# Attention outputs reach the output projection's layout through DRAM, with one inverse denominator row per head spread to 16 rows

## The chip, the cores and the metric

The kernel is one program on one core of a Trainium2 chip. Its time is the device time of one execution in microseconds (us). Before the change three runs gave 2191.11, 2204.84 and 2227.48 us; the median is 2204.84 us. The core has five engines that run their own instruction streams in order: TensorE (PE; its weight loads are shown apart as PEld), VectorE (DVE), ScalarE (ACT), GpSimd (POOL) and SyncE (SP, which here only issues transfers). They meet through semaphores.

## The reference, cut to what matters

The input is x of 4 batches, 1024 rows and 512 columns, all in float32. The block is a causal attention and then a mixture of experts, each between layer norms:

```python
# attention: 32 query heads of 16 columns, 8 key/value heads (each serves 4 query heads)
q, k = rope(x @ Wq), rope(x @ Wk);  v = x @ Wv
probs = softmax(causal(q @ k.T / sqrt(16)))
out = (probs @ v).transpose(0, 2, 1, 3).reshape(B, S, 512)    # head h is columns 16h .. 16h+15
attn = out @ Wo
x = x + layernorm(attn(layernorm(x)))
x = x + layernorm(moe(layernorm(x)))     # 64 experts, top 6, and a shared expert
```

The change concerns the two lines in the middle: the division of probs @ v by the sum of the exponentials, and the layout in which its result meets Wo.

## The kernel before, in words

The program has three phases: attention with everything that hangs on one row tile (out projection, layer norms, router, shared expert, dispatch of rows to experts), then 64 experts, then a final sum and layer norm. Only the first is touched. It ends about 1705 us into the execution.

Its attention works on 64 **items**: one batch, one half of its 512 query rows each, one key/value head with its four query heads. Per item, in order: SP loads the group's rotated rows (`load_group`, L613); ACT and POOL split them into high and low parts and PE turns them into columns; PE computes scores once (`score`, L822) so that DVE can take their row maxima (`reduce_unit`, L1265); the maxima are transposed (L840), copied by ACT (L1081) and put into the query tile as two extra rows by four small transfers (`place_maxima`, L624); PE computes the transposed scores (`scores_transposed`, L845), ACT takes the exponential (L1087), and PE multiplies by the values (`outputs`, L856).

The values carry 16 columns of ones beside their 16 columns. So a product has, per head, 32 rows on the partitions: 16 output rows and 16 equal rows with the sum of the exponentials (the denominator), each of 512 query columns. ACT copies it to SBUF (`copy_outputs`, L1096, tile `raw`).

From there the path to the output projection is, before the change:

- `raw_transpose` (L871): PE transposes `raw` in four blocks, so that query rows lie on the partitions again. One per item, 64 in all.
- `attended` (L1282): DVE takes the reciprocal of the 16 denominators of a row (L1289) and multiplies (L1291) into `an_g`.
- `store_attended` (L632): SP stores `an_g` into the item's 64 columns of a scratch tensor in DRAM.
- `load_attended` (L639): when the eight items of a half are stored, SP loads whole rows of 512 columns, one tile of 128 rows at a time, 32 in all.
- `attended_transpose` (L878): PE transposes the tile in four blocks; ACT copies it (`copy_anT`, L1103) into `anT`.
- `out_project` (L885): PE multiplies `anT` by Wo.

The order of the instructions on every engine is written out before the program is built, by a list scheduler (`Plan`, L115). Every step is an `op` with an engine, a duration, a due time (`aim`) and the steps that it follows; the scheduler takes, engine by engine, the step that can start first, shifted by its due time, and adds a lag for the result (`result_lag`, L290; 2.2 us for a transfer). It also hands out the eight PSUM banks. `H0` is the share of a batch's time that its first half is given; `ULEAD`, `ALEAD`, `ASTEP`, `CLAG`, `CSTEP0`, `CSTEP1` shift due times; `RESERVE` holds banks back. What stands in an engine's order is done in that order: a wait at the head of SP's order holds every transfer behind it.

## Time and profile before

| what | value |
|---|---|
| median of 3 runs | 2204.84 us |
| lowest, highest | 2191.11, 2227.48 us |
| profiled execution: its own time | 2203.77 us |
| its span in the trace | 2202.0 us |
| phase 1 (attention and rows) | 0 to about 1705 us |
| phase 2 (experts) | about 1705 to 2120 us |
| phase 3 (final sum) | 2120 to 2202 us |
| mean granted TensorE clock | 0.938 of 2.4 GHz |

A row that groups instructions gives their number, the engine's busy time with them and the mean duration of one, and then how long the engine was idle just before them and on whom it waited. A row of waits gives who waited, for whom, the total, the number of times and the longest. The chain of waits follows the work that ended last back to the start; what is on it sets the time. SPq is SP issuing a transfer.

### The profile page before, as it was taken

How to read it: one execution, taken by the hardware profiler on the slowest of the kernel's cores; microseconds unless marked ns; L12 is line 12 of the kernel's file. 1: busy time of each engine (PE TensorE's matmuls, PEld its weight loads, DVE VectorE, ACT ScalarE, POOL GpSimd, SP SyncE). 2: the span in 40 equal slices, each digit the busy share in tenths (PEclk: the TensorE clock that was granted, in tenths of full speed). 3: DMA queues.
4: the chain of work that ended last, by engine and by line, in shares of the span. 5: the costliest groups of instructions: out<-in, count | busy, mean ns of one | idle time of the engine just before them, and what ended most of it. 6: DMA issues, size and time to landing. Idle time of an engine off the chain costs nothing.

```text
span 2202.0 us, 37596 instructions
## 1 busy us (share of the span) xinstructions
PE 1912.8 (87%) x12579; PEld 922.6 (42%) x12579; DVE 1236.4 (56%) x2714; ACT 1160.7 (53%) x2592; POOL 904.8 (41%) x1209
## 2 busy tenths in 40 slices
PE   5989999999999999999999999999886888888820
PEld 3544344345444444444444544444332444444410
DVE  3455777656677765658777466787723111222248
ACT  1465577667657766665777766678642122222200
POOL 4744432345442354545433554343214122222248
PEclk9998999999999999999999999999988899999965
DMA  5565332222221122212111122111011999999988
GB/s 179 170 222 172 116 118 84 93 68 92 70 91 53 43 70 71 66 54 85 57 38 37 48 61 61 58 54 38 16 46 34 294 301 283 311 323 293 287 249 289
DMA packets 201642, 280.63 MB, mean 127 GB/s; under 512 B 109783, under 2 KB 109783, under 8 KB 201472
## 3 DMA queue, kind: packets, MB, share of 16 engines
q1 hardware_dynamic: 175152, 239.32, 33.4%
q0 software_dynamic: 24576, 35.07, 6.6%
q10 hardware_dynamic: 1744, 4.06, 0.5%
q8 instruction: 95, 1.56, 0.3%
q14 instruction: 75, 0.61, 0.1%
HBM read 168.85 MB, written 147.46 MB: 144 GB/s over the span
## 4 chain that ended last, share of the span: by engine, by line
PE 62%; DMA 11%; ACT 8%; DVE 7%; issue 5%; SPq 3%; POOL 2%; DVEq 1%; POOLq 1%; ACTq 0%
PE ps L867 11%; PE ps L831 7%; DMA gx<-dispatch_scratch 6%; PE ps L802 6%; ACT pr L1093 5%; PE ps L979 5%; PE ps L851 5%; PE ps L891 5%; PE ps L911 5%; PE ps L1011 3%; PE ps L918 3%; SPq L629 2%; PE ps L933 2%; DVE rmax L1275 2%; DMA qT<-mT 2%
## 5 line engine op out<-in xcount | busy, mean ns | idle before, releaser
L1275 DVE TENSOR_REDUCE rmax<-ps 128x1 f32<-128x512 f32 (+3 forms) x1280 | 735.3, 631 | 251.6 <-PE ps L836 164.3
L1093 ACT ACTIVATE pr<-ps 128x512 f32<-128x512 f32 (+3 forms) x1536 | 623.1, 513 | 169.1 <-PE ps L851 166.8
L831 PE MATMUL ps<-kT,qT 48*128 48x512 f16 (+3 forms) x1536 | 350.4, 337 | 24.5 <-DVE rmax L1275 14.4
L867 PE MATMUL ps<-pr,v_ones 128*32 128x512 f32 (+3 forms) x3072 | 334.7, 527 | 6.9 <-ACT pr L1093 2.8
L1572 POOL TENSOR_SCALAR_AFFINE_SELECT pr<-pr 128x512 f32<-128x512 f32 x256 | 163.8, 642 | 415.3 <-ACT pr L1093 414.7
L851 PE MATMUL ps<-qT,kT 50*128 50x512 f16 (+3 forms) x1536 | 301.7, 338 | 33.5 <-DMA qT<-mT 24.6
L1597 POOL DMA_INDIRECT dispatch_scratch<-x,slot_i x192 | 191.7, 999 | 143.9 <-DVE slot_i L1367 94.9
L1630 POOL DMA_INDIRECT acc_scratch<-eo,etok x64 | 98.8, 1543 | 309.6 <-DVE eo L1417 280.4
L831 PEld LDWEIGHTS ps<-kT,qT 48*128 48x128 f16 x1536 | 106.4, 93 | 274.0 <-ACT pr L1093 93.8
L979 PE MATMUL ps<-gu_sb,gxT 128*128 128x384 f32 x512 | 199.5, 515 | 0.0
L802 PE MATMUL ps<-wqkv_sb,xT 128*128 128x288 f32 (+1 forms) x512 | 181.4, 501 | 4.2 <-ACT xT L1048 4.2
L1408 DVE TENSOR_TENSOR eh<-ps,esg 128x192 f32<-128x192 f32 x64 | 22.9, 358 | 264.6 <-ACT esg L1190 264.6
L851 PEld LDWEIGHTS ps<-qT,kT 50*128 50x128 f16 x1536 | 95.1, 94 | 167.4 <-ACT pr L1093 86.7
L834 PE MATMUL ps<-above,sel 64*128 64x128 bf16 x1024 | 162.4, 219 | 0.0
L836 PE MATMUL ps<-above,sel 64*128 64x64 bf16 x1024 | 146.1, 189 | 0.0
L1180 ACT ACTIVATE gxT<-ps 128x512 f32<-128x512 f32 x64 | 38.2, 597 | 190.0 <-PE ps L986 177.2
L891 PE MATMUL ps<-wo_sb,anT 128*128 128x512 f32 x256 | 122.4, 622 | 4.0 <-ACT anT L1107 3.7
L802 PEld LDWEIGHTS ps<-wqkv_sb,xT 128*128 128x128 f32 x512 | 94.1, 192 | 67.0 <-issue 48.5
L1011 PE MATMUL ps<-dn_sb,ehT 96*128 96x512 f32 x256 | 120.6, 592 | 0.5 <-ACT ehT L1195 0.5
L867 PEld LDWEIGHTS ps<-pr,v_ones 128*32 128x32 f32 x3072 | 72.9, 112 | 96.9 <-issue 54.9
L979 PEld LDWEIGHTS ps<-gu_sb,gxT 128*128 128x128 f32 x512 | 93.3, 203 | 39.1 <-issue 8.2
L911 PE MATMUL ps<-shgu_sb,x2T 128*128 128x448 f32 x256 | 107.1, 562 | 1.5 <-ACT x2T L1119 1.4
(147 smaller groups left out, 2596.2 us busy)
## 6 DMA issues: line engine op xcount, KB each, us to landing
gu_sb<-w_gu_dram SPq DMA_DIRECT2D x64, 768.0 KB, 6.6
dn_sb<-w_dn_dram SPq DMA_DIRECT2D x64, 384.0 KB, 8.9
dispatch_scratch<-blank SPq DMA_DIRECT2D x64, 288.5 KB, 4.5
gx<-dispatch_scratch SPq DMA_DIRECT2D x64, 288.5 KB, 5.4
rotated_scratch<-qkv SPq DMA_DIRECT2D x32, 384.0 KB, 2.4
grp<-rotated_scratch SPq DMA_DIRECT2D x32, 384.0 KB, 3.6
xin<-x_dram SPq DMA_DIRECT2D x32, 256.0 KB, 3.2
xres<-x_dram SPq DMA_DIRECT2D x32, 256.0 KB, 2.8
```

The costliest lines, as they stand in the source:

```text
L802: last = pe.matmul(ps[:, bank_of["q", n, part], 0:cols[1] - cols[0]], xT[n % 2][:, c, :], wqkv_sb[:, c, cols[0]:cols[1]], start=c == 0, st ...
L831: last = pe.matmul(o, qT[it % 2][r:r + SROWS, h // 2, q % QPH * P:(q % QPH + 1) * P], kT[it % 2][r:r + SROWS, kh * HALF:kh * HALF + w], st ...
L851: pe.matmul(ps[:, bank_of["s", it, i, h], 0:HALF - c0], kT[it % 2][r:r + BROWS, kt * P:(kt + 1) * P], qT[it % 2][r:r + BROWS, h // 2, c0:H ...
L867: last = pe.matmul(ps[32 * h:32 * h + 32, bank_of["v", it], c0:HALF], v_ones[it % 2][:, kt, :], pr[k % SLOTS][:, h, 0:HALF - c0], start=kt ...
L891: last = pe.matmul(ps[:, bank_of["w", n], :], anT[:, c, :], wo_sb[:, c, :], start=c == 0, stop=c == DC - 1)
L911: last = pe.matmul(ps[:, bank_of["g", n], 0:E + SI], x2T[n % 2][:, c, :], shgu_sb[:, c, 0:E + SI], start=c == 0, stop=c == DC - 1)
L979: last = pe.matmul(gu, gxT[k % 2][:, c, :], gu_sb[k][:, c, :], start=c == 0, stop=c == DC - 1)
L1011: last = pe.matmul(ps[:, 4 + k % 2, :], ehT[k % 2][:, c, :], dn_sb[k][:, c, :], start=c == 0, stop=c == 1)
L1093: act.activation(pr[k % SLOTS][:, h, 0:HALF - c0], ps[:, bank_of["s", it, i, h], 0:HALF - c0], ACT.Exp, scale=factor).then_inc(exp_done, 1)
L1275: dve.tensor_reduce(dst[:, heads[0] % 2, heads[0] // 2:heads[0] // 2 + n, q % QPH], ps[:, bank_of["u", it, u], 0:n * w].rearrange("p (h k) ...
L1572: pool.affine_select(out=tile, in_=tile, compare_op=ALU.is_ge, fill=0.0, base=0, pattern=[[0, REP], [1, P]], channel_multiplier=-1).then_i ...
L1597: pool.indirect_dma_start(out=disp_d, out_offset=bass.IndirectOffsetOnAxis(ap=slot_i[:, n % 4, k:k + 1], axis=0), in_=x2[n % 4][:], in_off ...
```

## The change

The product with its denominators goes to DRAM as it is and comes back in the layout in which the output projection reads it. Step by step, for an item (`it`) and for a pair of items (`pp`, two neighbouring key/value heads, 128 of the 512 columns):

- `store_raw`: SP stores `raw` (128 rows of 2 KB) into a scratch tensor.
- `load_raw`: SP loads the 64 output rows of the item straight into `anT`, which now holds a half's 512 query columns and is doubled. It waits for the store, and at a half's start for the output projections that still read the buffer.
- `load_denominators`: SP loads one of the 16 equal denominator rows of each head, cut to 128 partitions of 16 numbers, into `den`.
- `invert`: DVE takes the reciprocal of a pair's denominators (128x32).
- `store_inverses`, `spread_inverses`: SP stores them in a second scratch tensor and loads them so that each head's row is repeated on 16 partitions, two transfers of 64 rows per pair.
- `attended`: DVE multiplies a pair's 128x512 block of `anT` in place.
- `out_project` waits for the four pairs of a half and reads `anT`.

Both transposes on PE, ACT's copy of `anT`, and the store and load of `an` are gone, and with them two of the kinds of PSUM banks. `copy_outputs` waits for the store of two items ago where it waited for the transpose. The planner gets the new steps, other numbers, and lags by kind of transfer.

```diff
-H0 = 0.32
+H0 = 0.244
-RESERVE = 3
+RESERVE = 2
-ULEAD = -0.186
-ALEAD = 0.066
-ASTEP = 0.1
-CLAG = 0
-CSTEP0 = 0.173
-CSTEP1 = 0.124
+ULEAD = -0.471
+ALEAD = 0
+ASTEP = 0.095
+CLAG = 0.03
+CSTEP0 = 0.146
+CSTEP1 = 0.086
...
-            op(s_rt, ("rt", it), "pe", 0.45, t_i + 2 * step, ("raw", it), bank=("r", it))
-            op(s_an, ("an", it), "dve", 0.67, t_i + 2.2 * step, ("rt", it), ("as", far) if far is not None else None, frees=("r", it))
-            op(s_as, ("as", it), "sp", 0.06, t_i + 3 * step, ("an", it))
+            op(s_as, ("as", it), "sp", 0.06, t_i + 2 * step, ("raw", it))
+            pp, end = divmod(it, 2)
+            op(s_nl, ("nl", it), "sp", 0.07, t_i + 4 * step, ("as", it), ("an", pp - 2) if pp >= 2 else None,
+               ("wo", it // KVH * QPH - QPH - 1) if it >= 2 * KVH else None)
+            op(s_dl, ("dl", it), "sp", 0.07, t_i + 3 * step, ("as", it), ("ds", pp - 2) if pp >= 2 else None)
+            if end:
+                op(s_ri, ("ri", pp), "dve", 0.30, t_i + 5 * step, ("dl", it - 1), ("dl", it))
+                op(s_ds, ("ds", pp), "sp", 0.07, t_i + 5.5 * step, ("ri", pp))
+                op(s_bl, ("bl", pp), "sp", 0.14, t_i + 6 * step, ("ds", pp), ("an", pp - 2) if pp >= 2 else None)
+                op(s_an, ("an", pp), "dve", 0.62, t_i + 7 * step, ("nl", it - 1), ("nl", it), ("bl", pp))
...
-            op(s_at, ("at", n), "pe", 0.44, at, ("al", n), ("wo", n - 1) if n else None, bank=("a", n))
-            op(s_atc, ("atc", n), "act", 0.48, at + e, ("at", n), frees=("a", n))
-            op(s_wo, ("wo", n), "pe", DC * 0.86, at + 3 * e, ("atc", n), ("x1", n - 2) if n >= 2 else None, bank=("w", n))
+            op(s_wo, ("wo", n), "pe", DC * 0.86, at + 3 * e, ("an", QPH * (n // QPH) + QPH - 1), ("x1", n - 2) if n >= 2 else None, bank=("w", n))
...
-        return {"sp": self.DMA, "act": 0.17, "dve": 0.09, "pool": 0.12}[engine]
+        if engine == "sp":
+            return {"gl": 3.8, "mr": 2.4, "rs": 2.8, "ds": 2.6, "cl": 4.5}.get(name[0], 3.2)
+        return {"act": 0.17, "dve": 0.09, "pool": 0.12}[engine]
...
-        rden = sb("rden", [P, QPH * REP], f32, att)
-        an_g = [sb(f"an_g{k}", [P, QPH, REP * HD], f32, att) for k in range(2)]
-        an = [sb(f"an{k}", [P, D], f32, att) for k in range(2)]
-        anT = sb("anT", [P, DC, P], f32, att)
+        den = [sb(f"den{k}", [P, 2, HD], f32, att) for k in range(2)]
+        inv = [sb(f"inv{k}", [P, HALF], f32, att) for k in range(2)]
+        anT = [sb(f"anT{k}", [P, DC, HALF], f32, att) for k in range(2)]
...
+        raw_t = raw_d.rearrange("(n p) q -> n p q", p=P)
+        raw_parts = raw_d.rearrange("(n h two d) q -> n two h d q", h=REP, two=2, d=HD)
+        den_parts = raw_d.rearrange("(n h two d) (j e) -> n two d h j e", h=REP, two=2, d=HD, e=HD)
+        inv_flat = inv_d.rearrange("(pp i h) (j e) -> pp (h j) i e", i=2, h=REP, e=HD)
+        inv_t = inv_d.rearrange("(n h) q -> n h q", h=REP)
...
+            def store_raw(it):
+                sp.wait_ge(pv_copied, it + 1)
+                sp.dma_start(raw_t[it], raw[it % 2][:]).then_inc(raw_out[it % 2], 16)
+
+            def load_raw(it):
+                sp.wait_ge(raw_out[it % 2], 16 * (it // 2 + 1))
+                if it >= 4:
+                    sp.wait_ge(an_ready, it // 2 - 1)
+                if it >= 2 * KVH:
+                    sp.wait_ge(wo_done, QPH * (it // KVH - 1))
+                rows = slice(ROWT * (it % 2), ROWT * (it % 2) + ROWT)
+                sp.dma_start(anT[it // KVH % 2][rows, it % KVH // 2, :], raw_parts[it, 0]).then_inc(raw_in[it // 2 % 2], 16)
+
+            def load_denominators(it):
+                pp = it // 2
+                sp.wait_ge(raw_out[it % 2], 16 * (it // 2 + 1))
+                if pp >= 2:
+                    sp.wait_ge(inv_out[pp % 2], 16 * (pp // 2))
+                sp.dma_start(den[pp % 2][:, it % 2, :], den_parts[it, 1, 0]).then_inc(den_in[pp % 2], 16)
+
+            def store_inverses(pp):
+                sp.wait_ge(inv_ready, pp + 1)
+                sp.dma_start(inv_flat[pp], den[pp % 2][:]).then_inc(inv_out[pp % 2], 16)
+
+            def spread_inverses(pp):
+                sp.wait_ge(inv_out[pp % 2], 16 * (pp // 2 + 1))
+                if pp >= 2:
+                    sp.wait_ge(an_ready, pp - 1)
                 for k in range(2):
-                    sp.wait_ge(an_out[k], 16 * (KVH // 2) * (n // QPH + 1))
-                if n >= 2:
-                    sp.wait_ge(t1_done, n - 1)
-                sp.dma_start(an[n % 2][:], an_t[n]).then_inc(an_in[n % 2], 16)
+                    sp.dma_start(inv[pp % 2][ROWT * k:ROWT * k + ROWT, :],
+                                 inv_t[2 * pp + k].unsqueeze(1).broadcast_to((REP, HD, HALF))).then_inc(raw_in[pp % 2], 16)
...
-                pe.wait_ge(anT_copied, n + 1)
+                pe.wait_ge(an_ready, QPH * (n // QPH + 1))
                 for c in range(DC):
-                    last = pe.matmul(ps[:, bank_of["w", n], :], anT[:, c, :], wo_sb[:, c, :], start=c == 0, stop=c == DC - 1)
+                    last = pe.matmul(ps[:, bank_of["w", n], :], anT[n // QPH % 2][:, c, n % QPH * P:(n % QPH + 1) * P], wo_sb[:, c, :],
+                                     start=c == 0, stop=c == DC - 1)
...
+            def invert(pp):
+                dve.wait_ge(den_in[pp % 2], 32 * (pp // 2 + 1))
+                dve.reciprocal(den[pp % 2][:], den[pp % 2][:]).then_inc(inv_ready, 1)
+
+            def attended(pp):
+                dve.wait_ge(raw_in[pp % 2], 64 * (pp // 2 + 1))
+                heads = anT[pp // (KVH // 2) % 2][:, pp % (KVH // 2), :]
+                dve.tensor_tensor(heads, heads, inv[pp % 2][:], ALU.mult).then_inc(an_ready, 1)
```

**SP's order, second half of the third batch** (L629/L639 place the maxima of an item, L621/L631 load a group, L636 stores `an_g`; L644 stores `raw`, L660 loads denominators, L653 loads outputs, L664 stores inverses, L657/L685 store the shared expert's rows). Before:

```order
L621 DMA grp0<-rotated_scratch 128x8x96
L629 DMA qT1<-mT1 1x8x128 x4
L636 DMA attended_scratch<-an_g0 128x4x64
L621 DMA grp1<-rotated_scratch 128x8x96
L629 DMA qT0<-mT0 1x8x128 x4
L636 DMA attended_scratch<-an_g1 128x4x64
```

Now:

```order
L639 DMA qT1<-mT1 1x8x128 x4
L631 DMA grp0<-rotated_scratch 128x8x96
L644 DMA raw_scratch<-raw0 128x512
L660 DMA den1<-raw_scratch 128x1x16
L653 DMA anT1<-raw_scratch 64x1x512
L685 DMA acc_scratch<-ysh0 128x512
L639 DMA qT0<-mT0 1x8x128 x4
L631 DMA grp1<-rotated_scratch 128x8x96
L644 DMA raw_scratch<-raw1 128x512
L660 DMA den1<-raw_scratch 128x1x16
L653 DMA anT1<-raw_scratch 64x1x512
L664 DMA inverse_scratch<-den1 128x2x16
```

Between two placements of maxima there stood one store of attention outputs; now there stand a store and two loads that wait for it, the first of them directly behind it, and in every second item the inverses' store and spread as well.

**DVE's order at one item of the third batch** (L1275/L1280 are the row maxima of the scores). Before:

```order
L1275 TENSOR_REDUCE rmax0<-ps 128x1 [waits sc_done]
L1289 RECIPROCAL rden<-ps 128x16 [waits an_ready,an_out0,raw_done]
L1291 TENSOR_TENSOR an_g0<-ps,rden 128x256
L1275 TENSOR_REDUCE rmax0<-ps 128x1 [waits sc_done] x2
L1327 TENSOR_REDUCE nmax<-ps 128x1 [waits pexp_ready,gate_done]
L1275 TENSOR_REDUCE rmax0<-ps 128x1 [waits sc_done] x6
```

Now:

```order
L1280 TENSOR_REDUCE rmax0<-ps 128x2 [waits sc_done]
L1290 RECIPROCAL den1<-den1 128x32 [waits den_in1]
L1280 TENSOR_REDUCE rmax0<-ps 128x2 [waits sc_done] x2
L1280 TENSOR_REDUCE rmax0<-ps 128x1 [waits sc_done] x8
L1296 TENSOR_TENSOR anT1<-anT1,inv1 128x512 [waits raw_in1]
L1299 BN_STATS cst6<-yo0 128x6 [waits wo_copied]
```

DVE's two instructions waited for a transpose on PE; now each of the pair's two waits for transfers, with score maxima in front, between and behind.

**PE's order at the end of phase 1** (L867/L897 are the last products with the values, L891/L907 the output projection, L898/L915 the transpose of the normed rows). Before:

```order
L867 MATMUL ps<-pr3,v_ones1 32x128 x4
L875 MATMUL ps<-id_f,raw1 128x128 x4
L882 MATMUL ps<-id_f,an0 128x128 x4
L891 MATMUL ps<-wo_sb,anT 128x512 x4
L882 MATMUL ps<-id_f,an1 128x128 x4
L891 MATMUL ps<-wo_sb,anT 128x512 x4
L882 MATMUL ps<-id_f,an0 128x128 x4
L891 MATMUL ps<-wo_sb,anT 128x512 x4
L898 MATMUL ps<-id_f,x20 128x128 x4
```

Now:

```order
L897 MATMUL ps<-pr3,v_ones1 32x128 x4
L907 MATMUL ps<-wo_sb,anT1 128x512 x12
L915 MATMUL ps<-id_f,x20 128x128 x4
L907 MATMUL ps<-wo_sb,anT1 128x512 x4
L928 MATMUL ps<-shgu_sb,x2T0 128x448 x4
```

Three projections stand in a row, with nothing of PE's or ACT's between them; all of them wait for the last pair of the half.

## Rows read from the trace of the kernel before

**Rows 1.** The page's busy times: engine, us, share of the span, instructions.
```profile
PE 1912.8 (87%) x12579; PEld 922.6 (42%) x12579; DVE 1236.4 (56%) x2714; ACT 1160.7 (53%) x2592; POOL 904.8 (41%) x1209
```

**Rows 2.** Windows: length, busy PE, PEld, DVE, ACT, POOL; clock, DMA share, GB/s.
```profile
60.00:1600.00 1540.00, 1458.10 (x11051) 682.04 (x11053) 1031.56 (x2231) 1032.67 (x2317) 673.03 (x1022) 0.96 0.25 79
1600.00:1705.00 105.00, 74.92 (x264) 33.08 (x256) 33.37 (x102) 34.49 (x66) 36.08 (x40) 0.86 0.13 42
```

**Rows 3.** PE's waits from 60 to 1600 us: total, times, longest.
```profile
PE ps L851 <- DMA qT<-mT: 24.6, 23, 2.8
PE ps L831 <- DVE rmax L1275: 14.4, 22, 3.1
...
PE ps L875 <- ACT raw L1101: 3.5, 7, 1.0
...
PE ps L882 <- DMA an<-attended_scratch: 1.8, 1, 1.8
...
PE ps L891 <- ACT anT L1107: 1.3, 4, 0.5
PE ps L831 <- DVE an_g L1291: 1.2, 3, 0.5
```

**Rows 4.** The chain of waits from 60 to 1600 us: shares by line, largest first.
```profile
by line: PE ps L867 16.2%; PE ps L831 9.6%; ACT pr L1093 7.5%; PE ps L851 7.4%; PE ps L802 6.2%; PE ps L891 6.0%; issue 5.6%; PE ps L911 5.6%; SPq L629 3.5%; PE ps L918 3.3%; DVE rmax L1275 3.2%; PE ps L933 3.1%; DMA qT<-mT 3.0%; PE ps L834
```

**Rows 5.** Timeline of PE near 1010 and 1018 us: start, duration, instruction.
```profile
1009.84 0.60 PE L875 MATMUL ps<-id_f,raw 128*128 128x128 f32 x4
1010.37 0.34 PE L831 MATMUL ps<-kT,qT 48*128 48x384 f16 x2
...
1018.01 0.60 PE L882 MATMUL ps<-id_f,an 128*128 128x128 f32 x4
1018.55 0.60 PE L831 MATMUL ps<-kT,qT 48*128 48x512 f16 x3
```

**Rows 6.** Instruction groups: count, busy us, mean ns, idle time before them.
```profile
L1275 DVE TENSOR_REDUCE rmax<-ps 128x1 f32<-128x512 f32 (+3 forms) x1280 | 735.3, 631 | 251.6 <-PE ps L836 164.3 <-PE ps L831 82.0 <-issue 0.2
...
L1291 DVE TENSOR_TENSOR an_g<-ps,rden 128x256 f32<-128x256 f32 x64 | 27.2, 425 | 4.8
...
L1107 ACT ACTIVATE anT<-ps 128x512 f32<-128x512 f32 x32 | 19.3, 604 | 26.3 <-PE ps L882 26.1
...
L1374 DVE TENSOR_TENSOR hid<-ps,sgm 128x384 f32<-128x384 f32 x32 | 17.7, 553 | 14.8 <-PE ps L918 8.5 <-issue 3.6 <-ACT sgm L1131 2.7
...
L1289 DVE RECIPROCAL rden<-ps 128x16 f32<-128x16 f32 x64 | 16.2, 254 | 94.1 <-PE ps L875 94.1
```

**Rows 7.** Timeline of SP's queue near 1025 us: start, duration of the issue, transfer.
```profile
1023.87 2.69 SPq L629 DMA_DIRECT2D qT<-mT  x4
1026.67 0.37 SPq L644 DMA_DIRECT2D an<-attended_scratch  x1
```

**Rows 8.** Transfers by line: number, size of one, median us to landing.
```profile
attended_scratch<-an_g SPq DMA_DIRECT2D x64, 128.0 KB, 2.0
...
an<-attended_scratch SPq DMA_DIRECT2D x32, 256.0 KB, 2.8
```

**Rows 9.** The chain of waits from 1500 to 1780 us, in order of time.
```profile
1567.89 1.72 DMA qT<-mT
...
1614.14 0.60 ACT raw L1101
...
1622.82 6.46 PE ps L891 x8
...
1630.53 3.69 PE ps L891 x8
```

**Rows 10.** Waits of SP's queue over the whole span.
```profile
SPq L629 <- ACT mT L1085: 338.6, 52, 21.0
```

**Rows 11.** Waits of DVE over the whole span.
```profile
DVE rden L1289 <- PE ps L875: 94.1, 33, 21.4
...
DVE st L1222 <- DMA xin<-x_dram: 37.8, 15, 5.9
```

More of the change, by code:

```diff
@@ L228, in build @@
                    ("mask", it, i) if diagonal(half, kt) else None, ("v", it) if i == 0 else None,
-                   ("rt", far) if i == 0 and far is not None else None, bank=("v", it) if i == 0 else None)
-            op(s_raw, ("raw", it), "act", 0.48, t_i + 1.2 * step, ("pv", it, NP[half] - 1), ("rt", far) if far is not None else None,
+                   bank=("v", it) if i == 0 else None)
+            op(s_raw, ("raw", it), "act", 0.48, t_i + 1.2 * step, ("pv", it, NP[half] - 1), ("as", far) if far is not None else None,
                frees=("v", it))
-            op(s_rt, ("rt", it), "pe", 0.45, t_i + 2 * step, ("raw", it), bank=("r", it))
-            op(s_an, ("an", it), "dve", 0.67, t_i + 2.2 * step, ("rt", it), ("as", far) if far is not None else None, frees=("r", it))
-            op(s_as, ("as", it), "sp", 0.06, t_i + 3 * step, ("an", it))
+            op(s_as, ("as", it), "sp", 0.06, t_i + 2 * step, ("raw", it))
[8 more added lines that the diff above has]
+                op(s_an, ("an", pp), "dve", 0.62, t_i + 7 * step, ("nl", it - 1), ("nl", it), ("bl", pp))
         s_cl = new()
@@ L545, in program @@
         pv_done, pv_copied = sem("pv_done"), sem("pv_copied")
-        raw_done, an_ready = sem("raw_done"), sem("an_ready")
-        an_out = [sem(f"an_out{k}") for k in range(2)]
-        an_in = [sem(f"an_in{k}") for k in range(2)]
-        t1_done, anT_copied, wo_done, wo_copied = sem("t1_done"), sem("anT_copied"), sem("wo_done"), sem("wo_copied")
+        raw_out = [sem(f"raw_out{k}") for k in range(2)]
+        raw_in = [sem(f"raw_in{k}") for k in range(2)]
+        den_in = [sem(f"den_in{k}") for k in range(2)]
+        inv_out = [sem(f"inv_out{k}") for k in range(2)]
+        inv_ready = sem("inv_ready")
+        an_ready, wo_done, wo_copied = sem("an_ready"), sem("wo_done"), sem("wo_copied")
         xres_in = [sem(f"xres_in{k}") for k in range(2)]
@@ L678, in _ @@
                 elif kind == "as":
-                    store_attended(*at)
-                elif kind == "al":
-                    load_attended(*at)
+                    store_raw(*at)
+                elif kind == "nl":
+                    load_raw(*at)
+                elif kind == "dl":
+                    load_denominators(*at)
+                elif kind == "ds":
+                    store_inverses(*at)
+                elif kind == "bl":
+                    spread_inverses(*at)
                 elif kind == "xr":
@@ L869, in outputs @@
                 last.then_inc(pv_done, 1)
-            def raw_transpose(it):
-                pe.wait_ge(pv_copied, it + 1)
-                free_bank(("r", it))
-                for t in range(QPH):
-                    last = pe.transpose(ps[:, bank_of["r", it], t * P:(t + 1) * P], raw[it % 2][:, t * P:(t + 1) * P], id_f[:])
-                last.then_inc(raw_done, 1)
-            def attended_transpose(n):
-                pe.wait_ge(an_in[n % 2], 16 * (n // 2 + 1))
-                free_bank(("a", n))
-                for c in range(DC):
-                    last = pe.transpose(ps[:, bank_of["a", n], c * P:(c + 1) * P], an[n % 2][:, c * P:(c + 1) * P], id_f[:])
-                last.then_inc(t1_done, 1)
             def out_project(n):
@@ L1099, in copy_outputs @@
                 if it >= 2:
[L1100 removed]
+                    act.wait_ge(raw_out[it % 2], 16 * (it // 2))
                 act.activation(raw[it % 2][:], ps[:, bank_of["v", it], :], ACT.Copy).then_inc(pv_copied, 1)
[L1103 to L1107 removed]
             def copy_wo(n):
```

51 lines of the change are left out of this document (9 added, 42 removed).

## The prediction, made before the changed kernel was timed

> **What bounds the kernel now.** I read the page's busy times first: PE 87%, the next engine 56% [rows 1]. The windows say where: from 60 to 1600 us PE is busy 1458.1 of 1540 us at a granted clock of 0.96 [rows 2]. So the stage that the change touches is filled by PE to 95%, and PE work taken out of it is worth something. The two later stages hold none of the changed steps; I leave them as they are.
>
> PE's waits come next: in those 1540 us the longest is for the rows of maxima, 24.6 us in 23 waits, then 14.4 us for DVE's score maxima [rows 3]. The chain of waits must be set against the 95%: ACT's exponentials (7.5%), issue (5.6%), SP's issues of the maxima (3.5%), DVE's maxima (3.2%) and the landing of the maxima (3.0%) make 22.8% of it [rows 4]. The reader is to see that PE looks nearly full while almost a quarter of the time is decided elsewhere.
>
> **The change part by part.** *Transposes of the raw product.* 64 groups of four. A group shows 0.60 us, but the next instruction starts 0.53 us after it [rows 5]; that spacing is what goes: 64 x 0.53 = 33.9 us. *Transposes of whole rows.* 32 groups, 0.54 us apart from the next [rows 5]; 28 lie before 1600 us: 15.1 us. Together 49.0 us of PE in the stage. The bounds are 49.0 (PE sets every moment) and what is left if the 22.8% outside PE absorbs its share: 49.0 x 0.772 = 37.8 us. I take 37.8, because the chain and not the busy share says what sets the end.
>
> *Waits that leave with them.* PE waited 3.5 us for `raw`, 1.8 for the loaded rows, 1.3 for ACT's `anT` and 1.2 for `an_g` [rows 3]: 7.8 us, gone. What is late next is the output projection itself, which now waits for the fourth pair of a half; except at the very end, PE has the next half's scores ahead of it, so I cost that at nothing. If that cover were gone it would be the end's price, below, up to seven more times.
>
> *ACT.* 28 copies of 0.604 us [rows 6] are 16.9 us; ACT's exponentials hold 7.5% of the chain [rows 4]: 1.3 us. *DVE.* Out: 64 x (0.254 + 0.425) = 43.5 us [rows 6]. In: 32 reciprocals of 128x32, between 0.254 and twice that (twice the columns), and 32 products of 128x512, by the 128x384 product 0.553 x 512/384 = 0.74 us [rows 6]; with 0.30 for the first, 33 us. Ten us less on an engine with 3.2% of the chain: nothing. DVE's wait for the raw transpose, 94.1 us in 33 places [rows 11], goes, and 64 waits for transfers take its place; behind each stand score maxima, as the order shows. DVE already waits 37.8 us for loaded rows in 15 places [rows 11], and PE's wait for the maxima is 14.4 us in all [rows 3]. So I let the new ones replace the old at no cost, and keep the other end for the rivals.
>
> *SP.* Out: 64 stores and 32 loads. In: 64 stores of `raw`, 64 loads of outputs, 64 of denominators, 32 stores of inverses and 64 spreads, 288 for 96. An issue takes 0.37 us for a plain tile and 2.69/4 = 0.67 for a placement of maxima [rows 7]; 192 more are 71 to 129 us of SP in 1540. That alone stops nothing: SP stood waiting for ACT's maxima in 52 of 64 items, 338.6 us [rows 10]. What counts is a transfer that waits for a landing with a placement of maxima queued behind it. In the new order 35 of 64 denominator loads stand directly behind the store that they read, and 14 of 32 spreads directly behind theirs. Of the 64 placements 9 come directly behind a load of outputs and 8 behind a spread: 17 behind a landing of 2.0 us (the store of 128 KB) [rows 8]. PE was kept waiting by 23 of 64 placements [rows 3], so 17 x 23/64 x 2.0 = 12 us. Bounds: 0, if SP always comes after the landing, and 70 us, if all 35 placements that directly follow a new step are 2.0 us late and PE waits each time. I stay near the low end, since SP was early in 52 of 64.
>
> *The end.* After the last copy of `raw` (ends 1614.74) the first projection began at 1622.82, 8.1 us later [rows 9]. Now: store 2.0, denominators 2.0, reciprocal 0.3, store 2.0, a first spread's issue 0.7, spread 2.8 (the 256 KB load), product 0.74 [rows 6, 7, 8]: 10.5 us, 2.4 later. Three projections then follow without the 1.25 us that lay between them (1629.28 to 1630.53) [rows 9], but the first tile's chain decides what follows, so I give no credit; with it the end would come out 1.4 us earlier.
>
> *Planner's numbers and banks.* They move nearly every step by a few places. Nothing in the trace prices that; I take 0, with 39 us as the most it could return on PE (the 24.6 and 14.4 us [rows 3]), and as much the other way.
>
> **Sum:** -37.8 - 7.8 - 1.3 + 12 + 2.4 = -32.5. The profiled execution took 2203.77 us (1.77 of it outside its span), 1.07 below the median of 2204.84: 2203.8 - 32.5 = **2171 us**, 1.5% under the median. Two per cent, about what a measurement of this kernel can tell from no change, is 44 us: faster means below 2160.7, slower above 2248.9.
>
> **The rivals.** *All of it counts.* If PE sets every moment, the gain is 49.0 + 7.8 + 1.3 - 2.4 = 55.7, with no loss on SP: 2148 us; if the new order also halves PE's two waits (39 us [rows 3]) it is 2129. For it: 95% busy. Against: the 22.8%. Chance 0.26.
>
> *The time comes back as a wait for the maxima.* A placement takes four issues, 2.69 us, and lands 1.72 us later [rows 7, 9]; none of that shrinks when PE has less to do, and an item gets shorter by about 0.8 us (49.0/64). If PE then waits 0.5 us longer in each of 64 items, 32 us return: 2203 us, no change. For it: 6.5% of the chain lies there already [rows 4]. Against: SP was early in most items [rows 10]. Chance 0.12.
>
> *Narrow transfers, slower than before.* The spread reads one row for 16 partitions, and outputs and denominators are read head by head, four at a time. If they ran on a quarter of the width that a 128-row tile has, their bytes would take four times as long. 128 KB land in 2.0 and 256 KB in 2.8 us [rows 8]: 0.8 us per 128 KB over a fixed 1.2. A pair's spread of 256 KB would land 1.2 + 4 x 1.6 = 7.6 us after issue, against 3.2 (and 0.14 for the issue) by which the planner places DVE's product. DVE then stands 4.3 us with score maxima behind it. The planner lets PE be two score units ahead, 1.3 us of reductions at 0.631 each [rows 6], so it loses up to 3.0 us a pair, 96 us in 32 pairs; in place of SP's 12 that is 2171 - 12 + 96 = 2255 us. It decides from a landing of about 7 us on. Against it: DVE's waits for landings did not show on PE before [rows 3, 11]. The Trainium skill bears on this, in DMA: Bandwidth & Descriptors, section Why a DMA increments its semaphore by 16 and not by 1: a transfer uses as many engines as divide both sides' slowest dimension, up to 16. By that rule these access patterns, whose slowest dimension on the DRAM side is 4 heads, would get 4 of 16, as this rival has it, and the time would be its 2255 us; no row here shows a transfer's width. Chance 0.11.
>
> *It does not save what it says:* not possible for the transposes, whose instructions are absent from the new order.
>
> **How the numbers follow.** The forecast has 0.51; its own range is 2145 to 2195 (SP's term from 0 to 34, the planner's numbers), a quarter of it below 2160.7. Faster by over 2%: 0.26 + 0.14 = 0.40. Slower: 0.11. Within 2%: 0.49. The range 2115 to 2240 holds the forecast, both its neighbours and most of the planner's scatter, and leaves out most of the slower case and the far end of the fast one.
>
> **What would show it.** In the new profile: no transposes of `raw` or `an`; PE busy from 60 us to the end of attention lower by about 49 us, and the stage shorter by less; PE's wait for maxima 25 to 40 us, not 70; DVE's waits for `inv` and `den` short, and not followed by a longer wait of PE for DVE's maxima; landings of the spread near 3 us; the first of the last four projections about 10.5 us after the last copy of `raw`. I am wrong if PE's busy time does not fall by its 49 us, if the stage shortens by all of it, or if the spread lands at 7 us and DVE stands for it.

## The result: slower by 2.2%, where 1.5% faster was forecast

| | before | after |
|---|---|---|
| median (range, runs), measured side by side | 2206.73 us (2191.11 to 2227.48, 4) | 2238.82 us (2225.98 to 2250.91, 4) |
| ratio to before, 95% interval | | 1.0225 [1.0143, 1.0307] |
| profiled execution: its time, span | 2203.77, 2202.0 us | 2232.23, 2230.5 us |
| last copy of `raw` begins | 1614.1 us | 1670.3 us |
| phase 1 ends (first load of an expert's rows) | 1707.5 us | 1754.7 us |
| mean granted TensorE clock | 0.938 | 0.912 |

The ratio is 50 us of 2206.73 us, against a forecast of -32.5. Its interval says that the change is slower, by 1.4 to 3.1%; whether by more than 2% it leaves open. Some executions of every kernel run longer than the rest: the ratios leave them out (the two medians alone differ by 32 us), and the profiles of `x_noden`, `x_pairlag`, `x_pairlag2` and `x_pairbusy` below are of such executions, so that the experiments use their first phase only. The profiled executions of the two kernels differ by 28.5 us in span, and phase 1 alone by 47, since the second phase was 17 us shorter after the change (last section); the last copy of `raw` comes 56 us later. So the time was lost where the change was made, before that copy.

The page's busy times of the kernel after (as in [rows 1]):

```profile
PE 1911.9 (86%) x12195; PEld 889.8 (40%) x12195; DVE 1229.7 (55%) x2650; ACT 1146.3 (51%) x2560; POOL 911.7 (41%) x1209
```

384 matmuls are gone and PE is as long busy as before: 1911.9 against 1912.8 us. The windows of the kernel after (columns as in [rows 2]), the second up to its last copy of `raw`:

```profile
60.00:1600.00 1540.00, 1419.24 (x10305) 637.94 (x10305) 993.43 (x2106) 980.03 (x2203) 663.38 (x997) 0.93 0.28 89
60.00:1670.30 1610.30, 1477.68 (x10768) 656.68 (x10767) 1027.71 (x2167) 1030.68 (x2315) 680.41 (x1025) 0.92 0.27 86
```

The kernel before did the same stretch of the program, up to 1614.1 us, in 1554.1 us with 1470.7 busy at a clock of 0.96. Now PE is idle for 132.6 us of 1610.3 instead of 83.4, and busy for 7 us more with some 49 us less to do, at 0.92. Both are new: more standing, and slower work. PE's longest waits before the last copy of `raw`, and DVE's two largest waits for transfers over the span, in the kernel after (who waited, for whom, total, times, longest; [rows 3, 11] are those before):

```profile
PE ps L881 <- DMA qT<-mT: 56.9, 35, 6.0
...
PE ps L861 <- DVE rmax L1280: 18.6, 47, 2.6
...
PE ps L943 <- DVE hid L1378: 9.9, 3, 4.1
```

```profile
DVE den L1290 <- DMA den<-raw_scratch: 47.0, 8, 27.9
DVE anT L1296 <- DMA inv<-inverse_scratch: 39.2, 18, 7.3
```

PE's wait for the maxima has grown from 24.6 to 56.9 us. DVE waits for the spread inverses in 18 of 32 pairs, 2.2 us each. Its wait for the denominators is larger in sum, but 27.9 us of it are one wait behind the last copy of `raw`, when DVE has nothing else to do, and `x_noden` below shows the rest to cost little. One of the waits for the spread, from the views of the kernel after, is the case in small. SP's queue, then DVE, then PE near 971 us (start, duration, instruction, in brackets the idle time before it and what ended it):

```profile
971.17 1.18 SPq L671 DMA_DIRECT2D inv<-inverse_scratch  x2
...
971.79 1.89 DVE L1280 TENSOR_REDUCE rmax<-ps 128x1 f32<-128x512 f32 x3 [0.48 <-PE ps L866]
976.81 0.69 DVE L1296 TENSOR_TENSOR anT<-anT,inv 128x512 f32<-128x512 f32 x1 [3.13 <-DMA inv<-inverse_scratch]
977.42 0.68 DVE L1280 TENSOR_REDUCE rmax<-ps 128x1 f32<-128x512 f32 x1
978.02 0.55 DVE L1378 TENSOR_TENSOR hid<-ps,sgm 128x384 f32<-128x384 f32 x1
...
978.72 0.88 PE L943 MATMUL ps<-id_f,hid 128*128 128x128 f32 x3 [3.62 <-DVE hid L1378]
```

The chain of waits of the same kernel names the transfer, and the windows (columns as in [rows 2]) show what PE does around it; the last of them is the 0.6 us before PE stands:

```profile
971.80 4.99 DMA inv<-inverse_scratch
```

```profile
970.00:975.00 5.00, 3.38 (x28) 1.30 (x24) 2.91 (x5) 4.97 (x11) 4.08 (x5) 0.95 0.65 197
975.00:980.00 5.00, 1.38 (x8) 0.70 (x11) 2.67 (x5) 1.34 (x5) 1.21 (x5) 0.50 0.22 69
980.00:985.00 5.00, 5.00 (x17) 1.60 (x10) 1.97 (x6) 1.24 (x6) 1.95 (x4) 0.52 0.34 106
985.00:990.00 5.00, 5.00 (x48) 2.19 (x47) 0.00 (x0) 2.98 (x7) 1.18 (x3) 1.00 0.14 53
...
974.50:975.10 0.60, 0.49 (x2) 0.10 (x1) 0.00 (x0) 0.60 (x3) 0.60 (x2) 0.51 0.29 106
```

The second half of the spread lands 4.99 us after its issue. DVE, next in order on the product, stands 3.13 us for it with score maxima and `hid` queued behind; PE runs out of other work and stands 3.62 us for `hid`; and from 975 to 985 us PE is granted 0.50 to 0.52, its lower level of 1.2 GHz, though from 980 on it is busy all the time. The level had fallen at about 974.5, 0.6 us before PE began to stand, so this one case does not show that the standing made it fall. Counted from the timelines up to the last copy of `raw`, PE stood for 2 us or longer at 4 places (11.5 us) before and at 15 (50.6 us) after. Five of the 15 (14.9 us) come behind a wait of DVE for the spread; nine (33.0 us) are waits for the placed maxima.

At the end of phase 1, the chain of the kernel after (as in [rows 9]) is longer than forecast too, most of all by its spread:

```profile
1670.88 2.01 DMA raw_scratch<-raw
...
1672.91 1.96 DMA den<-raw_scratch
...
1675.27 2.44 DMA inverse_scratch<-den
1678.32 4.17 DMA inv<-inverse_scratch
...
1682.51 0.70 DVE anT L1296
...
1683.35 9.38 PE ps L907 x16
```

From the end of the copy (1670.86) to the first projection it is 12.5 us; 8.1 before, 10.5 forecast.

### The profile page after: what moved, and what is told of

Same layout as the page of the kernel before. It is cut to its first block, busy times and chain, and to the rows that moved or that the text cites. A ratio compares the mean times of both kernels' runs of the same rounds, so it can differ in the third digit from the quotient of the medians.

```text
span 2230.5 us, 36788 instructions
## 1 busy us (share of the span) xinstructions
PE 1911.9 (86%) x12195; PEld 889.8 (40%) x12195; DVE 1229.7 (55%) x2650; ACT 1146.3 (51%) x2560; POOL 911.7 (41%) x1209
## 3 DMA queue, kind: packets, MB, share of 16 engines
q1 hardware_dynamic: 171824, 257.15, 34.9%
## 4 chain that ended last, share of the span: by engine, by line
PE 56%; DMA 15%; DVE 9%; ACT 6%; issue 5%; SPq 5%; POOL 2%; DVEq 1%; POOLq 1%; ACTq 0%
PE ps L897 11%; PE ps L861 6%; DMA gx<-dispatch_scratch 6%; PE ps L992 5%; PE ps L881 5%; PE ps L907 5%; PE ps L832 4%; ACT pr L1106 4%; PE ps L928 4%; DVE rmax L1280 4%; SPq L639 3%; PE ps L1024 3%; PE ps L950 3%; DMA qT<-mT 3%; DMA inv<-inverse_scratch 2%
## 5 line engine op out<-in xcount | busy, mean ns | idle before, releaser
L1280 DVE TENSOR_REDUCE rmax<-ps 128x1 f32<-128x512 f32 (+3 forms) x1280 | 731.7, 629 | 330.8 <-PE ps L866 205.9
L861 PE MATMUL ps<-kT,qT 48*128 48x512 f16 (+3 forms) x1536 | 362.8, 343 | 30.1 <-DVE rmax L1280 18.6
L881 PE MATMUL ps<-qT,kT 50*128 50x512 f16 (+3 forms) x1536 | 325.1, 347 | 70.8 <-DMA qT<-mT 56.9
L897 PE MATMUL ps<-pr,v_ones 128*32 128x512 f32 (+3 forms) x3072 | 344.7, 545 | 7.0 <-POOL pr L1578 3.3
L907 PE MATMUL ps<-wo_sb,anT 128*128 128x512 f32 x256 | 129.2, 654 | 17.5 <-DVE anT L1296 16.6
L897 PEld LDWEIGHTS ps<-pr,v_ones 128*32 128x32 f32 x3072 | 75.9, 114 | 116.8 <-issue 71.4
```

What stands on the lines that cost most here:

```text
L861: last = pe.matmul(o, qT[it % 2][r:r + SROWS, h // 2, q % QPH * P:(q % QPH + 1) * P], kT[it % 2][r:r + SROWS, kh * HALF:kh * HALF + w], st ...
L881: pe.matmul(ps[:, bank_of["s", it, i, h], 0:HALF - c0], kT[it % 2][r:r + BROWS, kt * P:(kt + 1) * P], qT[it % 2][r:r + BROWS, h // 2, c0:H ...
L897: last = pe.matmul(ps[32 * h:32 * h + 32, bank_of["v", it], c0:HALF], v_ones[it % 2][:, kt, :], pr[k % SLOTS][:, h, 0:HALF - c0], start=kt ...
L907: last = pe.matmul(ps[:, bank_of["w", n], :], anT[n // QPH % 2][:, c, n % QPH * P:(n % QPH + 1) * P], wo_sb[:, c, :], start=c == 0, stop=c ...
L1280: dve.tensor_reduce(dst[:, heads[0] % 2, heads[0] // 2:heads[0] // 2 + n, q % QPH], ps[:, bank_of["u", it, u], 0:n * w].rearrange("p (h k) ...
```

## The experiments

The theories: **A**, the transfers with four heads at a time are narrow and land late (the rival of 0.11). **B**, the way through DRAM costs it at any width, by its waits for landings in DVE's and SP's orders. **C**, the planner's new numbers and lags cost it. **D**, SP's waits for landings keep the placements of the maxima waiting. **E**, the new order as such costs it, through the clock that PE is granted. The sharpest measure is the start of the last copy of `raw` in the profile (here `raw`), since the second phase, which no edit touches, scatters by itself (last section). Each kernel has one profile; the one kernel that was profiled twice gave 1624.4 and 1623.0. In the diffs the ends of lines that do not change are left off.

| run | `raw` | phase 1 ends | PE busy, idle up to `raw` | clock | PE's wait for maxima | ratio to before, 95% |
|---|---|---|---|---|---|---|
| before | 1614.1 | 1707.5 | 1470.7, 83.4 | 0.96 | 24.6 | 1 |
| after | 1670.3 | 1754.7 | 1477.7, 132.6 | 0.92 | 56.9 | 1.0225 [1.0143, 1.0307] |
| x_wide | 1638.3 | 1720.0 | 1463.7, 114.6 | 0.94 | 54.7 | 0.9985 [0.9899, 1.0072] |
| x_spread1 | 1649.2 | 1731.4 | 1464.6, 124.6 | 0.93 | 59.5 | 1.0101 [1.0059, 1.0144] |
| x_nospread | 1628.3 | 1707.0 | 1460.1, 108.2 | 0.94 | 56.9 | 0.9893 [0.9824, 0.9963] |
| x_noden | 1621.3 | 1699.3 | 1460.3, 101.0 | 0.94 | 45.9 | 0.9877 [0.9776, 0.9978] |
| x_plan | 1651.7 | 1744.2 | 1507.2, 84.5 | 0.94 | 25.3 | none; medians 2257.28, 2197.32 |
| x_oldnum | 1732.5 | 1817.0 | 1487.6, 184.9 | 0.92 | 70.6 | 1.0424 [1.0343, 1.0504] |
| x_wlag | 1627.9 | 1709.5 | 1462.4, 105.5 | 0.94 | 53.2 | 0.9945 [0.9881, 1.0009] |
| x_wfit | 1634.7 | 1716.4 | 1486.6, 88.2 | 0.94 | 16.4 | 1.0035 [0.9973, 1.0096] |
| x_pair | 1623.5 | 1705.8 | 1452.5, 111.0 | 0.94 | 53.9 | none; medians 2201.93, 2196.67 |
| x_pairlag | 1624.4 | 1706.3 | 1463.9, 100.5 | 0.94 | 49.1 | 0.9899 [0.9843, 0.9955] |
| x_pairlag2 | 1623.0 | 1704.9 | 1461.9, 101.1 | 0.94 | 49.3 | 0.9941 [0.9892, 0.9991] |
| x_pairbusy | 1661.9 | 1745.8 | 1505.3, 96.6 | 0.94 | 45.6 | 1.0119 [1.0029, 1.0208] |

**x_wide: the same transfers, 16 rows wide.** Within an item's 64 rows the partitions are ordered by column and then head, so that the slowest dimension of outputs and spread in DRAM is 16; the rows of Wo are permuted to match. Orders, sizes and counts stay.

```diff
-raw_d.rearrange("(n h two d) q -> n two h d q", h=REP, two=2, d=HD)
+raw_d.rearrange("(n h two d) q -> n two d h q", h=REP, two=2, d=HD)
...
-inv_t[2 * pp + k].unsqueeze(1).broadcast_to((REP, HD, HALF))
+inv_t[2 * pp + k].unsqueeze(0).broadcast_to((HD, REP, HALF))
```

> The rows of a pair are put on the partitions in another order (16 positions, then 4 heads), and Wo's rows with them; number, size and order of all transfers stay. Theory A (the loads of outputs and the spread are narrow: they read four heads at a time, land in 4 to 5 us and hold what is behind them): the spread lands in about 2.8 us, DVE's wait for it falls from 39 to under 15 us, PE's wait for the maxima from 57 to about 35, and the time to 2190 to 2205 us. Theory B (what costs is that SP waits in order for landings, however wide): less than 10 us change, 2228 to 2245. Theory C (the planner's numbers make the difference): no change.

The last spread's landing in its chain:

```profile
1645.58 2.87 DMA inv<-inverse_scratch
```

2.87 us instead of 4.17, DVE's wait for the spread 13.0 us in 5 places instead of 39.2 in 18, `raw` 32 us earlier, and 0.024 of the ratio (53 us) back. A holds: width is most of the loss. PE's wait for the maxima, which I expected near 35 us, stayed at 54.7. By the Trainium skill, DMA: Bandwidth & Descriptors, section Why a DMA increments its semaphore by 16 and not by 1, the form with 4 would use 4 of 16 engines and this one 16. The spreads' landings go the way of that rule, though not by the factor of four: on the chains of waits they took 4.2 to 5.7 us (11 spreads) in the kernel after and 2.7, 2.9, 3.6 and 5.0 us here. No row shows how many engines carried one.

**x_spread1: only the spread wide.** It reads one head's row for all 64 partitions; the outputs are still read four heads at a time. (Every head is divided by the first head's denominators: that is what is left out.)

```diff
-inv_t[2 * pp + k].unsqueeze(1).broadcast_to((REP, HD, HALF))
+inv_t[2 * pp + k, 0:1].broadcast_to((ROWT, HALF))
```

> The changed kernel, only the spread reads one head's row 64 times in place of four rows 16 times (so the other heads are divided by the wrong sums); number, bytes, places and the loads of outputs stay. If the spread is what the narrow patterns cost (DVE stands for it), two thirds or more of the 50 us between the change and the wide form come back: 2195 to 2215 us, DVE's wait for the spread under 15 us. If the loads of outputs, which lie in front of other transfers, cost as much: half, 2210 to 2225 us.

`raw` at 1649.2 is 21 of the 32 us, DVE's wait for the spread 22.6 us, above the 15 that I expected. So by `raw` two thirds of the width's price hang on the spread (by the ratios, 0.012 of 0.024, half), and the rest on the outputs' loads.

**x_nospread: no spread at all.** The product multiplies by ones (the division is left out); every order stays.

```diff
 elif kind == "bl":
-    spread_inverses(*at)
+    pass
```

> The change with its two spreads per pair left out (the product multiplies by ones; the division by the denominators is what is left out); the inverses are still formed and stored, the order of every engine is that of the change, and the loads of outputs and denominators stay four heads wide. If the spread's landing behind DVE's product is the main loss, most of the 32 us by which the wide form's last raw copy came earlier returns here and more, since the 2.9 us landing goes too: last raw copy 1625 to 1640 us, PE's wait for maxima still 45 to 60 us, ratio 0.99 to 1.00. If the narrow loads of outputs and denominators cost as much as the spread, the last raw copy stays above 1650 us and the ratio at 1.01.

PE's waits up to its last copy of `raw`, and the window:

```profile
PE ps L881 <- DMA qT<-mT: 56.9, 38, 7.6
...
PE ps L861 <- DVE rmax L1282: 10.1, 36, 0.6
...
PE ps L943 <- DVE hid L1380: 1.7, 2, 1.3
```

```profile
60.00:1628.30 1568.30, 1460.12 (x10773) 648.36 (x10771) 1027.78 (x2167) 1030.70 (x2315) 684.65 (x1027) 0.94 0.26 84
```

42 us come back, 24.4 as less idle time and 17.6 as less busy time at a clock of 0.94 instead of 0.92: the two halves that 971 to 985 us showed in small. PE's waits for DVE (`rmax`, `hid`) shrink by 16.7 us, its wait for the maxima not at all; so it is not SP's issues of the spreads and its waits ahead of them that count, which went as well and would show there. The end of phase 1 comes 48 us earlier. The ratio falls by 0.033 (73 us, with intervals of 18 us either way for the change and 15 here) to 0.9893, just under the range I had written; what lies beyond the 48 us is in the later phases or in the scatter, and is not located. Of the 56 us by which `raw` was late, the spread is the main part.

**x_noden: no way of the denominators at all** (again multiplied by ones, the division left out; loads of denominators, reciprocals, stores and spreads are gone).

```diff
 elif kind == "dl":
-    load_denominators(*at)
+    pass
```

> Leaves out the denominators' way: no load of denominators, no reciprocal, no store and no spread of inverses; DVE multiplies by ones once the outputs are loaded. Everything else keeps its place in the order. Theories A and B: 44 to 60 us are given back, 2170 to 2195 us, PE's wait for the maxima near the 25 us of the kernel before, the clock back to 0.95 or 0.96. Theory C: 2220 us or more.

`raw` is 7 us earlier than in `x_nospread`, and the ratios agree. What B has beyond the spread is small: once nobody waits for the spread, the loads of denominators, the reciprocals and the inverses' stores cost 7 us by `raw` and nothing that the ratios tell. PE's wait for the maxima (45.9 us) and the clock (0.94) did not come back to the 25 us and the 0.95 that I expected here: the denominators' way is not what raised the one and lowered the other.

**x_plan and x_oldnum: the numbers and the structure apart.** `x_plan` is the kernel before with the change's numbers and lags (the diff, cut), `x_oldnum` the change with the old ones.

```diff
-H0 = 0.32
+H0 = 0.244
...
-ULEAD = -0.186
+ULEAD = -0.471
```

> The kernel before with the change's planner numbers and lags, and its own path through the transposes. Theories A and B: within 1% of the kernel before, 2185 to 2225 us. Theory C: slower by most of what the change lost, 2230 us or more.

> The changed kernel with the planner numbers and the one lag of 2.2 us of the kernel before. Theories A and B: not faster than the change, 2235 to 2270 us, since a shorter assumed landing makes SP wait more. Theory C: 2200 us or less.

The window of `x_plan`:

```profile
60.00:1651.70 1591.70, 1507.18 (x11135) 693.89 (x11133) 1037.98 (x2231) 1044.84 (x2343) 676.60 (x1026) 0.94 0.24 76
```

The numbers suit only the structure that they come with. With the old ones the change is worse (`raw` 62 us later, DVE's wait for the spread 85.4 us in 28 places), so C falls in the form "the old numbers would have saved it". But on the structure before, the new order puts `raw` 37.6 us later with the same idle time (84.5 against 83.4 us): PE is longer busy with the same work, at 0.94 instead of 0.96. An order can cost PE's clock without adding to its idle time; that speaks for a part of E. It rests on this one profile: the runs of `x_plan` gave no ratio.

**x_wlag and x_wfit: SP reaches its waits later.** Both are `x_wide` with other planner's times. `x_wlag` takes 6.0 us for the store of `raw`; `x_wfit` takes issue times and lags from the traces.

```diff
-return {"gl": 3.8, "mr": 2.4, "rs": 2.8, "ds": 2.6, "cl": 4.5}.get(name[0], 3.2)
+return {"gl": 3.8, "mr": 2.4, "rs": 2.8, "ds": 2.6, "cl": 4.5, "as": 6.0}.get(name[0], 3.2)
```

```diff
-op(s_mr, ("mr", it), "sp", 0.15,
+op(s_mr, ("mr", it), "sp", 2.7,
```

> The wide form, and the planner believes that a store of the raw product lands 6.0 us later (3.2 before), so that the two loads behind it come later in SP's order. Theory D (SP's waits for landings hold the maxima, 109 us in 47 places): SP's wait for that store falls under 30 us, PE's wait for the maxima from 55 to 35 us, time 2170 to 2182 us. Theory E (the order of PE's work as such costs the clock, whatever SP does): PE's wait for maxima stays above 45 us and the time within 8 us of the wide form's 2188.

> The wide form with the planner's SP durations and lags set to measured ones (a placement of maxima 2.7 us of SP and 1.5 to land where it believed 0.15 and 2.4; 0.6 for a load, 1.2 for the two spreads). Theory D: the maxima are asked for sooner, PE's wait for them falls to 20 to 35 us, time 2160 to 2180 us. Theory E: the due times were chosen for the other durations, so a new order is as likely worse: 2180 to 2230 us.

The first cut SP's wait for the stores of `raw` from 109.0 to 74.8 us and brought `raw` 10 us forward. The second cut PE's wait for the maxima to a third:

```profile
PE ps L881 <- DMA qT<-mT: 16.4, 9, 4.2
```

```profile
60.00:1634.70 1574.70, 1486.55 (x10771) 659.65 (x10769) 1031.24 (x2167) 1030.26 (x2314) 682.28 (x1026) 0.94 0.28 89
```

Yet `raw` came only 3.6 us earlier: 26 us less idle, 23 us more busy, by the ratio no gain. The clock is 0.94 in both, so the added busy time is not the clock's; what it is no run here shows. D falls as the main cause: the largest of PE's waits can go and the time stays.

**x_pair and x_pairlag: a version against both kernels.** One load of outputs, one of denominators and one spread per pair, in the wide form: six transfers instead of nine. `x_pairlag` adds the 6.0 us.

```diff
-sp.dma_start(anT[it // KVH % 2][rows, it % KVH // 2, :], raw_parts[it, 0])
+sp.dma_start(anT[2 * pp // KVH % 2][:, 2 * pp % KVH // 2, :], raw_parts[pp, 0])
...
-    for k in range(2):
-        sp.dma_start(inv[pp % 2][ROWT * k:ROWT * k + ROWT, :], inv_t[2 * pp + k].unsqueeze(1).broadcast_to((REP, HD, HALF)))
+    sp.dma_start(inv[pp % 2][:], inv_t[pp].unsqueeze(0).broadcast_to((HD, 2 * REP, HALF)))
```

> The wide form with one load of outputs, one of denominators and one spread for a pair of items: 6 transfers a pair in place of 9, the same bytes. Theory D: 96 issues of 0.58 us and half of the waits for the store go, PE's wait for maxima 30 to 45 us, time 2165 to 2182 us. Theory E: within 8 us of the wide form's 2188, or either way by the new order.

> The wide form with one load of outputs, one of denominators and one spread per pair, and the planner's lag for the store of raw at 6.0 instead of 3.2 us, so that SP reaches the loads behind it later. If SP's waits for landings hold the maxima back and set the time, the two gains add: the last raw copy comes near 1613 us (1638 in the wide form, 15 less for six transfers in place of nine, 10 less for the lag), phase 1 ends near 1695, and the ratio to the kernel before is 0.985 to 0.995. If the time is set by the order as such and the clock that PE is granted (0.94 in each of the wide forms), nothing adds: the last raw copy stays at 1623 to 1640 us, SP's wait for the store of raw falls below 60 us all the same, and the ratio is 0.995 to 1.005.

`x_pair` brings `raw` 15 us forward from `x_wide`; the lag adds nothing to it (1624.4), though SP's wait for `raw`'s stores falls from 69.9 to 52.6 us. Phase 1 then ends where it did before the change. `x_pairlag` is the best version that does the whole work: 0.9899 and, once more, 0.9941, both intervals below 1. It beats both kernels, the one before by 0.6 to 1.0%.

**x_pairbusy: the removed PE work put back as idle work** into `x_pairlag`: 64 and 32 groups of four transposes of a constant, into banks that are overwritten at once. Orders, waits and transfers stay.

```diff
 free_bank(("v", it))
+for t in range(QPH):
+    pe.transpose(ps[:, bank_of["v", it], t * P:(t + 1) * P], id_f[:], id_f[:])
...
 free_bank(("w", n))
+for t in range(QPH):
+    pe.transpose(ps[:, bank_of["w", n], t * P:(t + 1) * P], id_f[:], id_f[:])
```

> The kernel with one set of transfers per pair and the 6.0 us lag, with the PE work that the change removed put back as idle work: 64 groups of four 128x128 transposes of a constant ahead of the products with the values, 32 ahead of the output projections, into banks that are overwritten at once. No order, wait or transfer changes. By the prediction's first step (PE's 49 us count by 0.77), the last raw copy comes 38 us later than in the same kernel without them (about 1662 against 1624) and the ratio to it is 1.017. If PE sets every moment it is 49 us, and 1.022. If the work removed was only turned into waits for the maxima and into a lower granted clock, those give most of it back: the last raw copy moves by less than 20 us, PE's wait for maxima falls from 49 us to 25 or less, and the granted clock of the stage stands at 0.95 or 0.96 again.

> The same kernel without the idle work, once more, as the other side of that comparison and for a second sum against the kernel before: by its first runs the ratio is 0.984 to 0.996 and the last raw copy comes at 1620 to 1630 us. If the ratio of those runs was chance, it is 0.996 to 1.005 here. The length of the second phase, which none of these edits touches, is 371 to 427 us in the runs so far; if it hangs on the execution and not on the kernel, it differs by over 10 us from that kernel's first profile, where it took 419 us.

The windows up to `raw` of `x_pairlag` and of `x_pairbusy`:

```profile
60.00:1624.40 1564.40, 1463.86 (x10771) 651.29 (x10769) 1032.70 (x2167) 1029.96 (x2315) 683.82 (x1026) 0.94 0.28 89
```

```profile
60.00:1661.90 1601.90, 1505.30 (x11138) 689.45 (x11136) 1033.31 (x2167) 1029.93 (x2315) 682.75 (x1025) 0.94 0.27 87
```

`raw` comes 37.5 us later, 38.9 by `x_pairlag2`; the ratios differ by 0.0178, 39 us. The first step's 37.8 us is what was measured, though here by adding work to `x_pairlag`, not by taking it off the kernel before. PE's wait for the maxima hardly moved (45.6 against 49.1 us), and the clock stayed at 0.94: nothing was given back. So the work that the change takes off PE is worth what I said, and E in the form "less work, lower clock" falls; what stays of it is that the new order runs at 0.94.

## Why the prediction was wrong, step by step

The sign was wrong: 2171 against 2238.82 us, by the ratio 50 us slower than before instead of 32.5 faster. **The step that failed is DVE's**, in its words: "So I let the new ones replace the old at no cost". Without the spread for which DVE waits, the last copy of `raw` comes 42 us earlier and phase 1 ends 48 us earlier (`x_nospread`). I had compared totals of waiting (94.1 us leaving, 64 waits coming [rows 11]) and not what stands behind each: behind the new ones stand the next score maxima and `hid`, and PE then stands too.

My argument against this rival, that DVE's waits for landings did not show on PE before [rows 3, 11], misread the trace. They did show: three of the four places where PE stood for 2 us or longer in the kernel before are such waits of DVE, for row tiles, with score maxima behind them. One of them (start, duration, instruction, idle time before it), and its windows:

```profile
415.36 0.69 DVE L1222 BATCH_NORM_STATS2 st<-xin 128x6 f32<-128x512 f32 x1 [3.17 <-DMA xin<-x_dram]
...
416.46 2.48 DVE L1275 TENSOR_REDUCE rmax<-ps 128x1 f32<-128x512 f32 x4
...
417.20 0.60 PE L831 MATMUL ps<-kT,qT 48*128 48x512 f16 x1 [3.09 <-DVE rmax L1275]
```

```profile
413.00:416.70 3.70, 1.07 (x8) 0.19 (x2) 1.19 (x4) 2.56 (x5) 0.08 (x1) 1.00 0.47 130
416.70:423.50 6.80, 6.30 (x29) 1.06 (x29) 5.32 (x9) 3.94 (x8) 0.49 (x1) 0.50 0.15 60
```

The three (3.12, 2.46 and 3.09 us) are 8.7 of the 14.4 us that [rows 3] gives as a total, and behind this one PE is granted 0.50 for 6.8 us. Followed from one such wait to PE, the trace of the kernel before had both halves of the loss.

This step is about half of the error. Up to the last copy of `raw` the terms (-37.8 - 7.8 - 1.3 + 12) make -34.9, and 1670.3 - 1614.1 = 56.2 was measured: 91 us apart, of which the spread is 42. Of the other 49, 7 go with the rest of the denominators' way (`x_noden`). The remainder no run assigns; the term that stood at 0 without a row is the planner's numbers, and `x_plan` shows that a new order can cost that much.

- *Transposes, -37.8:* the number is right, 37.5 to 39 us when the work is put back; its two factors less so. PE's busy time rose by 41.4 us there, not by 49.0, and 37.5 of these 41.4 came out, 0.91 and not 0.772. That the product fits is in part luck. "All of it counts" (49.0) did not hold.
- *The narrow rival:* right in mechanism, too large in size. It took 7.6 us for the landing and 96 us for the loss; the landings were 4.2 to 5.7 us and DVE's waits 2.2 us each in 18 of 32 pairs. The 7.6 takes a pair's 256 KB as one transfer; by the same estimate one spread of 128 KB is 1.2 + 4 x 0.8 = 4.4 us. Its turning point, "a landing of about 7 us", was too high: 5 us was enough, since DVE often comes to the product early. Its chance of 0.11 was too small for what its sentence on access patterns already said.
- *The rival of the maxima:* its 32 us are what PE's wait for the maxima grew by (24.6 to 56.9), but not for its reason, less work on PE: with the work put back the wait stays at 45.6 us (`x_pairbusy`). And that wait can go without the time (`x_wfit`).
- *SP, +12:* mis-sized as a wait. It took 2.0 us for the store of `raw`, the row of a 128 KB store; `raw` is 256 KB, and its stores landed after 2.9 us (median in the kernel after). PE's wait for the maxima grew by 32 us, 20 more than the term, while 25 to 40 us in all was forecast. But it is no price by itself, as `x_wfit` shows; six transfers for nine (`x_pair`) brought 15 us.
- *The planner's numbers, 0:* unproven in the change itself, but `x_plan` shows that a new order alone can move `raw` by 37.6 us, within my 39 and the other way than I leaned.
- *The end, +2.4:* +4.4, by a spread of 4.17 us instead of 2.8.
- *Signs named beforehand:* no transposes, as said; PE's busy time down by 49 us, wrong (38.9 less from 60 to 1600 us, where less of the program fitted in, and 7 more up to `raw`), because the clock fell, which I had not priced.

What stays open: without the spread, `raw` still comes 14 us later than before, where the removed work should bring it some 38 earlier. By the table that is some 25 us more idle time and a clock of 0.94 instead of 0.96; (1470.7 - 49) x 0.96/0.94 is 1452 us of busy time, 30 more than at 0.96, and 1460 was seen. Which steps of the new order cost that clock no run here singles out. Nor is the 1% by which `x_nospread` and `x_pairlag` beat the kernel before located: phase 1 ends at the same time in all three, and whether the second phase of the kernel before is longer as a rule its one profile cannot tell.

## What to carry to other kernels

When a step on PE is replaced by a trip through DRAM, price the work taken out (37.8 us forecast, 37.5 to 39 measured), and then go through the engines that wait for the landings: for each wait, what is queued behind it, and who needs that within the landing's time. Look in the trace before for one wait of that kind and follow it to PE; a total does not show it. Write a spread or a transposing load so that its slowest dimension is 16 and not 4; reordering the contraction's rows, with the weights' rows to match, costs nothing in the kernel and gave back 53 of the 82 us between forecast and result by the ratios (by `raw`, 32 of 91). And a stall of PE can cost more than its length (6.8 us at 0.50 behind 3.09 us at 417 us before, 17.6 us of busy time beside 24.4 of standing in `x_nospread`), so look at the granted clock around it before calling it small.
